# Two conv layers, attention and two expert layers on one core: a deeper pipeline where the second conv layer turns its elements into tokens

## What is computed

```python
def _L1_conv_ref(x, Wt, Wp, Wg, Ww, gamma, beta):
    ...
    out = jnp.einsum('bijl,cl->bijc', st, Ww) + x
    mean = out.mean(axis=(0, 1, 2))
    var = out.var(axis=(0, 1, 2))
    return (out - mean) * jax.lax.rsqrt(var + BN_EPS) * gamma + beta
...
t = _to_tokens(x)
t = t + _L2_attn_ref(_ln_t(t), L2_attn_W_qkv, L2_attn_W_o)
```

## Time and profile before

| | |
|---|---|
| median of 3 runs | 2285.59 us (2285.51 to 2291.93) |
| the profiled execution | 2278.83 us |
| its span, first to last instruction | 2277.1 us |
| busy: PE, DVE, ACT, POOL | 89%, 71%, 57%, 31% |
| mean granted TensorE clock | 0.941 of full speed |
| the stage that the change touches | 273.56 to 296.76 us |

### The profile page before, as it was taken

The page is one execution under the profiler, slowest core; times in us unless marked ns, Lnnn a source line. Parts: engine busy times, 40 slices in busy tenths (PEclk is TensorE's granted clock), DMA queues, the critical chain, the costliest instruction groups (busy, mean ns, idle before and its releaser), DMA issues. The chain is left out here.

```text
span 2277.1 us, 43941 instructions
## 1 busy us (share of the span) xinstructions
PE 2017.7 (89%) x15328; PEld 1626.0 (71%) x15328; DVE 1619.4 (71%) x3064; ACT 1286.6 (57%) x2255; POOL 711.8 (31%) x689
## 2 busy tenths in 40 slices
PE   6969776999988899989998658999984799999997
PEld 5858643566656788989998324666572699999997
DVE  3867765888847776756665677888757777777775
ACT  3434442777754444355554544777731488888885
POOL 1423200223320000068776001323300155555553
PEclk8989987999999999999999788999997899999999
DMA  4000015222203200055555442222115377777773
GB/s 130 1 0 0 0 52 134 59 57 61 60 17 123 78 19 19 19 109 119 101 98 68 134 112 70 61 55 61 36 42 171 118 230 230 226 214 214 229 227 85
DMA packets 176887, 218.59 MB, mean 96 GB/s; under 512 B 34169, under 2 KB 152610, under 8 KB 176354
## 3 DMA queue, kind: packets, MB, share of 16 engines
q1 hardware_dynamic: 146402, 175.19, 24.9%
q0 software_dynamic: 30336, 41.44, 10.9%
HBM read 161.25 MB, written 54.79 MB: 95 GB/s over the span
## 5 line engine op out<-in xcount | busy, mean ns | idle before, releaser
L1511 ACT ACTIVATE L_attn_probs<-L_attn_ps_t 128x512 f32<-128x512 f32 x640 | 359.5, 597 | 77.3 <-PE L_attn_ps_t L1428 68.3
L1410 PE MATMUL L_attn_ps_m<-L_attn_k,L_attn_q 96*128 96x512 bf16 (+3 forms) x1024 | 275.9, 310 | 29.9 <-DMA L_attn_k<-L_k_parts 28.3
L1375 POOL TENSOR_SCALAR_AFFINE_SELECT L_attn_probs<-L_attn_probs 128x512 f32<-128x512 f32 x256 | 153.2, 634 | 411.4 <-ACT L_attn_probs L1511 411.4
L1428 PE MATMUL L_attn_ps_t<-L_attn_q,L_attn_k 98*128 98x512 bf16 (+3 forms) x1024 | 246.6, 302 | 5.6 <-ACT L_attn_probs L1511 4.3
L2694 POOL DMA_INDIRECT out<-L_experts_result,L_moe_give x78 | 161.3, 2068 | 208.4 <-DVE L_experts_result L2866 196.5
L1412 PE MATMUL L_attn_ps_m<-L_attn_causal,L_attn_ident 128*128 128x128 bf16 x1024 | 198.6, 225 | 0.0
L2712 PE MATMUL L_experts_ps_y<-L_experts_w_high,L_experts_hT_low 128*128 128x256 f32 x624 | 179.9, 288 | 0.0
L2712 PE MATMUL L_experts_ps_h<-L_experts_xT_high,L_experts_w_low 128*128 128x256 f32 x624 | 178.1, 285 | 0.0
L2713 PE MATMUL L_experts_ps_h<-L_experts_xT_high,L_experts_w_high 128*128 128x256 f32 x624 | 177.9, 285 | 0.0
L2714 PE MATMUL L_experts_ps_h<-L_experts_xT_low,L_experts_w_high 128*128 128x256 f32 x624 | 177.7, 285 | 0.0
L2714 PE MATMUL L_experts_ps_y<-L_experts_w_low,L_experts_hT_high 128*128 128x256 f32 x624 | 176.8, 283 | 0.0
(11 more groups left out here) (456 smaller groups left out, 6078.0 us busy)
## 6 DMA issues: line engine op xcount, KB each, us to landing
L_staged_w<-L_ffn_w SPq DMA_DIRECT2D x78, 1024.0 KB, 5.7
L_attn_q<-L_q_parts SPq DMA_DIRECT2D x64, 192.0 KB
L_attn_q<-L_q_parts SPq DMA_DIRECT2D x64, 128.0 KB
L_moe_rows<-L_wo_normed SPq DMA_DIRECT2D x16, 512.0 KB, 2.9
L_q_parts<-L_qkv_q_parts SPq DMA_DIRECT2D x32, 192.0 KB, 2.9
L_q_parts<-L_qkv_parts SPq DMA_DIRECT2D x32, 192.0 KB, 3.4
load_rows<-x SPq DMA_DIRECT2D x8, 512.0 KB, 7.4
L_attn_q<-L_q_parts SPq DMA_DIRECT2D x64, 64.0 KB
```

Source lines behind the costliest of these rows:

```text
L1375: return pool.affine_select(out=block, in_=block, compare_op=ALU.is_ge, fill=0.0, base=0, pattern=columns, channel_multiplier=-1)
L1410: pe.matmul(bank[:, at:at + width], q[j][0:96, head, qb * P:(qb + 1) * P], k[j][0:96, 0:width], start=True, stop=False)
L1428: last = pe.matmul(bank[:, at:at + width], k[j][0:98, kb * P:(kb + 1) * P], q[j][0:98, head, kb * P:S], start=True, stop=True)
L1511: act.activation(probs[j % 2][:, place[unit], :], ps_t[:, n % 2, :], ACT.Exp, scale=scale).then_inc(exped, 1)
```

## The change

The two `normed` buffers go. Four buffers of the same size are cut out of the two `mixed_full` buffers, which nobody reads any more by then. All three loops of the stage are written out. ACT and VectorE normalise three elements before the first output, and then element b behind the output of element b-3; normalising b waits for the transposes of element b-4. PE's conditions stay as they were: both halves normalised, and element b-2 copied out.

```diff
@@ -279,10 +279,11 @@
         xb_parts = parts_of("xb", [P, KC, S])
-        normed = [sb(f"normed{p}", [P, KC, S]) for p in range(2)] if to_tokens else None
         theta, phi, g = parts_of("theta", [P, S]), parts_of("phi", [P, S]), parts_of("g", [P, TB, LAT])
         mixed_full = [sb(f"mixed_full{p}", [P, TB, S]) for p in range(2)]
         mixed = parts_of("mixed", [P, TB, S])
+        normed = [mixed_full[p][:, h * KC:(h + 1) * KC, :] for p in range(2) for h in range(TB // KC)]
+        RING = len(normed)
...
                 if to_tokens:
-                    def turn(b, p, first):
+                    for b in range(B):
                         pe.wait_ge(bn_done_a, b + 1)
                         pe.wait_ge(bn_done_v, b + 1)
-                        if not first:
+                        if b >= 2:
                             pe.wait_ge(bn_copied, b - 1)
-                        dst = (ps_out, ps_s)[p]
+                        dst = (ps_out, ps_s)[b % 2]
...
-                                                    normed[p][:, c, t * P:(t + 1) * P], net.ident[:, :])
+                                                    normed[b % RING][:, c, t * P:(t + 1) * P],
+                                                    net.ident[:, :])
                         last.then_inc(bn_turned, 1)
-                    turn(0, 0, True)
-                    turn(1, 1, True)
-                    with pe.Fori(1, B // 2) as i:
-                        for p in range(2):
-                            turn(i * 2 + p, p, False)
...
-                    def norm0(b, p, first):
-                        if not first:
-                            act.wait_ge(bn_turned, b - 1)
-                        act.activation(normed[p][:, 0, :], net.xT[:, 0, ds(b * S, S)], ACT.Identity,
+                    def norm0(b):
+                        if b >= RING:
+                            act.wait_ge(bn_turned, b - RING + 1)
+                        act.activation(normed[b % RING][:, 0, :], net.xT[:, 0, b * S:(b + 1) * S], ACT.Identity,
                                        bias=shift[:, 0:1], scale=scale[:, 0:1]).then_inc(bn_done_a, 1)
...
-                    norm0(0, 0, True)
-                    norm0(1, 1, True)
-                    with act.Fori(1, B // 2) as i:
-                        for p in range(2):
-                            take(i * 2 + p - 2, p)
-                            norm0(i * 2 + p, p, False)
-                    take(B - 2, 0)
-                    take(B - 1, 1)
+                    for b in range(B + 3):
+                        if b >= 3:
+                            take(b - 3)
+                        if b < B:
+                            norm0(b)
...
-                    norm1(0, 0, True)
-                    norm1(1, 1, True)
-                    with dve.Fori(1, B // 2) as i:
-                        for p in range(2):
-                            stats_of(i * 2 + p - 2)
-                            norm1(i * 2 + p, p, False)
-                    stats_of(B - 2)
-                    stats_of(B - 1)
+                    for b in range(B + 3):
+                        if b >= 3:
+                            stats_of(b - 3)
+                        if b < B:
+                            norm1(b)
```

More of the change, by code:

```diff
@@ L486, in _, with take @@
                 else:
-                    def norm0(b, p, first):
-                        if not first:
-                            act.wait_ge(bn_turned, b - 1)
-                        act.activation(normed[p][:, 0, :], net.xT[:, 0, ds(b * S, S)], ACT.Identity,
+                    def norm0(b):
+                        if b >= RING:
+                            act.wait_ge(bn_turned, b - RING + 1)
+                        act.activation(normed[b % RING][:, 0, :], net.xT[:, 0, b * S:(b + 1) * S], ACT.Identity,
                                        bias=shift[:, 0:1], scale=scale[:, 0:1]).then_inc(bn_done_a, 1)
-                    def take(b, p):
+                    def take(b):
                         act.wait_ge(bn_turned, b + 1)
-                        act.activation(net.x[:, ds(b * TB, TB), :], (ps_out, ps_s)[p][:, :, :].rearrange(
+                        act.activation(net.x[:, b * TB:(b + 1) * TB, :], (ps_out, ps_s)[b % 2][:, :, :].rearrange(
                             "p b (t c) -> p (b t) c", c=C), ACT.Copy).then_inc(bn_copied, 1)
-                    norm0(0, 0, True)
-                    norm0(1, 1, True)
-                    with act.Fori(1, B // 2) as i:
-                        for p in range(2):
-                            take(i * 2 + p - 2, p)
-                            norm0(i * 2 + p, p, False)
-                    take(B - 2, 0)
-                    take(B - 1, 1)
+                    for b in range(B + 3):
[3 more added lines that the diff above has]
+                            norm0(b)
             @block.gpsimd
@@ L621, in _, with norm1 @@
                 else:
[L622 to L625, removed]
+                    def norm1(b):
+                        if b >= RING:
+                            dve.wait_ge(bn_turned, b - RING + 1)
+                        dve.tensor_scalar(normed[b % RING][:, 1, :], net.xT[:, 1, b * S:(b + 1) * S], scale[:, 1:2], shift[:, 1:2],
                                           ALU.mult, ALU.add).then_inc(bn_done_v, 1)
```

## The result

The changed kernel took 2273.1 us (median of 6 runs, 2270.07 to 2277.07) where the kernel before, now with six runs, had 2285.55 (2282.39 to 2291.93): ratio 0.9955, 95% interval 0.9943 to 0.9967. Measured again on two other occasions, beside more runs of before, the ratio was 0.9974 (0.9960 to 0.9987) and 0.9967 (0.9955 to 0.9978), a gain some two thirds of the first.

A forecast was written before the change was run, and what follows sets the result against it. The prediction saw a ring of waits between VectorE, ACT and PE ending the second conv layer, VectorE bounding afterwards. Stage gain 4.5 us, between 4.1 and 4.9, other terms nothing: 2285.6 - 4.5 = 2281.1 us, range 2276.0 to 2287.5.

The forecast's parts named there:

- a ring of three engines: End of second conv layer: VectorE, ACT and PE wait for each other, 5.53 us from element 0 to element 2.
- the new waits: From element 4 on, normalising b waits for the transposes of element b-4; claimed cost nothing.
- the third normalising: Extra normalising at the stage's start, 0.53 us on VectorE and 0.80 on ACT, claimed hidden in idle time; nothing added.
- The rival in which the order wasn't the limit: Part of the rival with period 2.4 us and only 1.4 us gained, 2284.2 us; chance 0.14 for the whole rival.
- VectorE: ... 1.96 us per element: VectorE's period in the stage once elements are normalised ahead: 1.33 + 0.63 us, slowest engine and so the bound.
- less than the sum: Rival: hand-overs add to each element or order isn't the limit; period 2.4 us, gain 1.4, total 2284.2; chance 0.14.
- the two sums for the clock: Stage gain of 4.1 us with PE turns of 1.94, 4.9 with the last turn at 1.09; 4.5 taken.
- Statistics 0 start at 277.86 as before: Start of the stage's sum: VectorE's first token statistics were claimed not to move.
- The rival in which the clock gives more in the next two stages: Full PE clock in this stage, layer norm and first projection: 8.6 us less together, 2277.0 us; chance 0.12.
- Loops written out: I take nothing.: PE, ACT and VectorE lose one loop each in the stage: nothing to 0.3 us gained, counted as nothing.
- The base: 2285.59: Median of three runs of the kernel before, 6.8 us above the profiled execution; the 4.5 us gain was subtracted from it.
- 0.08 of the forecast's cases: Share for runs lying as low as the profiled one, added to the 0.12 for faster by over 0.3%.

The follow-up runs named there:

- the delay: Changed kernel plus eleven unused statistics instructions on VectorE behind the last token statistics: 2280.10 and 2281.07 us, ratios 0.9997 and 0.9996 to before.

## Why the prediction was wrong

**What held.** The mechanism: a ring of three engines taken apart by one more normalising ahead, VectorE the bound afterwards, its only long wait the one before the first copy, the new waits and the third normalising free, and the memory free. The rival in which the order wasn't the limit is refuted by three ahead with the loops kept (17.09 us) and by its opposite, two ahead with four buffers (21.08 us).

**The step that failed: "VectorE: ... 1.96 us per element".** This was read from statistics at 277.86, normalising at 279.19 and statistics at 279.82, as if VectorE had run freely. The third of these had waited. The copy ahead of it stands in the same timeline of the kernel before:

```profile
278.55 1.02 ACT L495 ACTIVATE x_tokens<-L_ps_s 128x1024 f32 x1 [0.28 <-issue]
```

It ended at 279.57, and 0.25 us of hand-over later, at 279.82, the statistics began. VectorE's own step from a normalising to the next statistics is 0.44 us, not 0.63. The sentence that held against the rival 'less than the sum', that elements 0 and 1 lay ready and followed each other at 1.96, rests on the same reading: element 1's copy was not ready. No pair in the first profile has a copy that came in time, so the step itself isn't in it; that the row had waited is. The second profile of before has such a pair:

```profile
283.12 0.53 DVE L625 TENSOR_SCALAR L_normed<-conv_x_channels,L_norm 128x512 f32 x1
283.56 1.40 DVE L244 BATCH_NORM_STATS2 x_stats<-x_tokens  x4
```

With 1.76 the prediction's own sum is 277.86 + 5 x 1.76 + 4.01 (twelve statistics in a row, which it had as 3 x 1.41) = 290.67, 6.1 us less instead of 4.9, and three ahead with the loops kept measured just this. Term by term, the stage fell by 6.46 us where 4.5 was forecast: 1.0 of the difference is the period (five times 0.20), 0.2 the twelve statistics, 0.4 the choice of a value between the two sums for the clock, and 0.4 the start, where "Statistics 0 start at 277.86 as before" didn't hold (3.92 us after the first normalising instead of 4.30). The ACT period suffered from the same fault: 1.85 read, 1.61 run (278.28 to 279.89).

**The clock in the stage** went the way of the higher sum. With the low clock to the end, the last turn would have set the end at about 291.8 by the same arithmetic, a gain of 4.9 instead of 6.1. All eight profiles with three ahead and no delay, and both with one, have one stretch at the low clock of 6.8 us in the stage; before had 10.2 and 6.8. The earlier turns didn't need it: in the changed kernel VectorE's period was 1.78 from the first statistics to the second (276.00 to 277.78), while the turns still took 1.76 to 1.97 us. In the kernel before, PE's idle times in mid stage were 1.9 and 1.8 us; now PE turned three elements without a pause and then idled 0.7 us between turns. The Trainium skill's rule on the clock gate ("TensorE: Matmul & The Clock Gate", "What's actually happening") had pointed this way with "sustained activity", and the trace agrees as far as the clock rose behind these three turns. That it stayed up with the pauses behind them is seen too; no run varied PE's pauses alone, so what decides it is not shown.

The rival in which the clock gives more in the next two stages is left open by the first profile alone and answered by the later ones. The first projection's eight products took 5.40 us before. In the changed kernel they took 3.70 in the first profile and 5.36 in the third (5.24 in the second):

```profile
309.34 3.70 PE L797 MATMUL L_qkv_ps_q<-L_moe_x_channels,L_qkv_w 128*128 128x512 f32 x8 [2.37 <-DVE L_qkv_w L862]
```

```profile
310.55 5.36 PE L797 MATMUL L_qkv_ps_q<-L_moe_x_channels,L_qkv_w 128*128 128x512 f32 x8 [2.38 <-DVE L_qkv_w L862]
```

The granted clock over the 3.8 us from the start of these products was 1.00 in the first of these profiles and 0.55 in the third. Both profiles with two ahead and the loops written out have 3.70 as well. So these 1.7 us differ between executions of one kernel and don't come reliably with the change.

**"Loops written out: I take nothing."** The term is 0.35 us with three ahead, and 2 us with two ahead: in the ring three hand-overs per two elements are on the path, and once the ring is open only those of the first element are. The rule on taken branches (the Trainium skill, "Runtime: NRT & Kernel Launch", "Instruction fetch mechanics") would have made the term larger by a stall at the branch. The trace showed a single packet in the whole stage, a loop kept on VectorE runs at 1.77 us per element against 1.76, and the 2 us with two ahead are the hand-overs; no run here shows such a stall.

**The base: 2285.59.** The largest part of the miss is not the change. Of the 8.0 us between forecast and result, the stage makes 2.0 and this base 4.2; the other 1.8 are not traced to a place (see below). It was a median of three. Over 103 later runs on three chips before has a median of 2281.4 and a mean of 2281.5, with single runs from 2276.4 to 2291.4. The profiled 2278.83 was more typical than the three runs: 21 of the 103 lie below it, and 93 below 2285.51, the lowest of the three. The 4.2 us went into the forecast, and the first comparison (12.4 us) carried them too. Why it lay high stays open. Three more runs of before at the first comparison gave 2282.39 to 2285.81, so that the median of six was still 2285.55; six runs this high together are unlikely as chance if they are drawn like the 103, and the record doesn't say on which chip they ran. The changed kernel's first six runs have the same mean as its later ones (2273.4 and 2273.6). The prediction saw that the three lay 6.8 over the profiled run. Set against that run, its own sum gave 2274.3, but the range from 2276.0 left this out, and "0.08 of the forecast's cases" for it was far too few.

**What stays open.** Means over all runs with the standard error: before 2281.5 (0.3, 103 runs), changed 2273.6 (0.5, 24), three ahead with loops 2272.6 (0.7, 12), with the delay 2280.2 (0.5, 23), two ahead with loops out, both kernels, 2279.4 (0.7, 23). The change gives 7.9 us with a standard error of 0.6, or 0.35%, and its stage only 6.2 to 6.5. With two ahead and the loops out, 2.1 us (0.8) are gained in the total and the same in the stage. With the delay, 6.5 us in the stage, the mean rises by 6.6 over the changed kernel's and stays 1.3 (0.6) under before's, so the surplus doesn't seem to hang on when the rest begins. In the mean granted clock before spent 276 us at 1.2 GHz and the changed kernel 263; the stage accounts for 10 of these 13 us. The rest would be worth 1 to 2 us, but where it lies is not shown. From the projection's second group of eight products to the end, the eight profiles with three ahead and no delay took 1951.7 to 1958.5 us, mean 1954.1, the two with the delay 1951.7 and 1955.1, and the four with two ahead 1952.5 to 1959.6, mean 1957.0. The difference of 2.9 us of the means has a standard error of 1.9, so chance isn't excluded, and no run shows what would cause it. The first comparison's larger gain is no evidence for it, since it rests on the high base.

## What to carry to other kernels

Before a period is read from two rows, look at when each of its inputs was ready: a row without idle time in brackets can still have waited, as the one at 279.82 did for 0.2 us. Where engines wait for each other in a ring, normalise one more element ahead in the queue order; if the order stays, more buffers do nothing. What a written-out loop is worth depends on whether its hand-overs are on the path: 2 us in the ring, 0.35 outside it. Where the gain is under half a per cent, the base needs dozens of runs from more than one occasion: the median of three was off by half of the gain, and that of six as well.

## What the runs showed of the hardware

- From a copy on ACT to the waiting statistics on VectorE passed 0.27 to 0.28 us in a loop and 0.03 to 0.04 written out. In the loop both the wait's value and the addresses come from registers, and no run separates the two. With the input ready in time VectorE's period was 1.77 us in the loop and 1.76 without.
- PE's eight transposes of 128x128 in f32 took 1.91 to 1.97 us at the granted clock of 0.50, or 1.71 to 1.79 from one eight to the next, and 1.04 to 1.09 at 1.00.
- The granted clock rose at 278, behind 5.05 busy us of PE in 6, and stayed up with PE busy 5.30 of the next 11 us; in the kernel before it stayed at 0.50 for ten us with PE busy 7.18 of them.
- The length of time at 1.2 GHz varies between executions of one program: from 264 to 302 us by the mean clock in the 103 runs of before, with 2276.4 and 2291.0 us at the two ends, some 0.4 us of time for each us at the low clock.
- GpSimd's 128x512 normalising took 0.77 us beside VectorE's statistics and 1.23 beside VectorE's normalising, which slowed down too (three in 1.76 us instead of 1.46).
